# Moving the square root of the RMS norm to the start of ScalarE's next step in a fused attention and MoE kernel

## The reference

```python
h = _layernorm(x) * (1 + ca) + sa
x = x + ga * attn(h)            # linear attention with decay, 16 heads of 16
h = _layernorm(x) * (1 + cb) + sb
x = x + gb * ffn(h)             # shared gated MLP + top 2 of 8 experts

# attn, after the block recurrence over n has made o:
o = o * rsqrt(mean(o * o, axis=-1) + 1e-6)
o = u * o
return o @ W_out.T
```

## Time and profile before

| | |
|---|---|
| median of 3 runs | 375.64 us (375.27 to 375.65) |
| profiled execution, its own time | 375.64 us |
| its span | 373.8 us |
| TensorE busy | 362.9 us, 97% |
| VectorE, ScalarE, GpSimd busy | 280.2, 218.6, 200.8 us |
| granted TensorE clock | 1.0 of full speed throughout |

### The profile page before, as it was taken

The page is one execution under the profiler, slowest core; times in us unless marked ns, Lnnn a source line. Parts: engine busy times, 40 slices in busy tenths (PEclk is TensorE's granted clock), DMA queues, the critical chain, the costliest instruction groups (busy, mean ns, idle before and its releaser), DMA issues.

```text
span 373.8 us, 12932 instructions
## 1 busy us (share of the span) xinstructions
PE 362.9 (97%) x4978; PEld 315.0 (84%) x4983; DVE 280.2 (75%) x561; ACT 218.6 (58%) x453; POOL 200.8 (54%) x193
## 2 busy tenths in 40 slices
PE   8989998999999989999999999999999999999996
PEld 4546555778888769899999999999999999999995
DVE  7996388999899985579976987777777675555543
ACT  5688667677677755648276746555555634333222
POOL 2000003978778785311364687868767787674240
PEclk9999999999999999999999999999999999999999
DMA  8956031000197007999425465574685865665443
GB/s 265 375 63 60 2 134 37 2 4 30 32 353 184 31 31 265 330 336 271 88 92 108 104 110 104 95 118 88 104 109 91 100 101 103 100 114 77 70 58 113
DMA packets 53043, 45.35 MB, mean 121 GB/s; under 512 B 31524, under 2 KB 46996, under 8 KB 52856
## 3 DMA queue, kind: packets, MB, share of 16 engines
q1 hardware_dynamic: 43048, 32.09, 32.5%
q0 software_dynamic: 7488, 10.27, 18.2%
q10 hardware_dynamic: 2448, 2.18, 1.8%
HBM read 27.60 MB, written 10.49 MB: 102 GB/s over the span
## 4 chain that ended last, share of the span: by engine, by line
PE 72%; POOL 13%; DVE 7%; issue 5%; ACT 3%; ACTq 0%; POOLq 0%; DVEq 0%
PE ps L1630 37%; PE ps L1648 18%; PE ps L1413 7%; POOL tmp L554 3%; POOL tmp L558 2%; POOL tmp L575 2%; PE ps L1399 2%; POOL h2s L579 2%; POOL tmp L573 2%; POOL wx L563 2%; PE ps L1341 2%; DVE st L937 1%; PE ps L1533 1%; PE ps L1361 1%; DVE tmp L1254 1%
## 5 line engine op out<-in xcount | busy, mean ns | idle before, releaser
L1630 PE MATMUL ps<-tmp,wx 128*128 128x128 bf16 x1776 | 105.5, 219 | 0.0
L1630 PEld LDWEIGHTS ps<-tmp,wx 128*128 (+1 forms) x1776 | 102.3, 98 | 0.9 <-issue 0.2
L611 POOL DMA_INDIRECT out<-tmp,dk x39 | 72.0, 1846 | 38.0 <-SPq L515 32.5
L857 ACT ACTIVATE tmp<-tmp 128x512 bf16<-128x512 f32 x55 | 34.6, 629 | 80.8 <-PE ps L1648 61.6
L1648 PE MATMUL ps<-wx,tmp 128*128 (+1 forms) x660 | 80.7, 273 | 0.2 <-DVE tmp L1260 0.2
L1648 PEld LDWEIGHTS ps<-wx,tmp 128*128 128x128 bf16 x660 | 62.2, 98 | 6.9 <-DVE tmp L1260 0.5
L1254 DVE TENSOR_TENSOR tmp<-ps,tmp 128x512 f32<-128x512 f32 x55 | 37.9, 689 | 37.7 <-PE ps L1630 32.1
L1630 PE MATMUL ps<-w_hl,wx 128*128 128x128 bf16 x864 | 51.3, 219 | 0.9 <-ACT tmp L846 0.9
L606 POOL DMA_INDIRECT tmp<-h2rows,src_i x39 | 42.1, 1081 | 16.7 <-issue 10.8
L1630 PEld LDWEIGHTS ps<-w_hl,wx 128*128 (+1 forms) x864 | 49.6, 98 | 1.4 <-issue 1.0
L1260 DVE TENSOR_TENSOR tmp<-tmp 128x512 bf16<-128x512 f32 x55 | 38.3, 696 | 10.1 <-ACT tmp L857 9.9
(11 more groups left out here) (194 smaller groups left out, 555.2 us busy)
## 6 DMA issues: line engine op xcount, KB each, us to landing
wx<-in_wexp SPq DMA_DIRECT2D x26, 512.0 KB, 5.4
xres<-in_x SPq DMA_DIRECT2D x4, 512.0 KB, 6.6
h2rows<-h2s ACTq DMA_DIRECT2D x16, 128.0 KB, 3.4
out<-h2s SPq DMA_DIRECT2D x12, 128.0 KB, 2.1
h2s<-in_wmod SPq DMA_DIRECT2D x1, 1024.0 KB, 9.5
wx<-decay_rows SPq DMA_DIRECT2D x16, 64.0 KB
modr<-mod_rows SPq DMA_DIRECT2D x1, 1024.0 KB, 4.4
wx<-in_wqkvu SPq DMA_DIRECT2D x1, 768.0 KB, 6.8
```

The lines of the kernel that those rows point to most:

```text
L611: e.indirect_dma_start(t["out"], bass.IndirectOffsetOnAxis(ap=dst_i[:, j:j + 1], axis=0), yb[(NA + j) % 2], None, compute_op=ALU.add).then ...
L857: e.activation(hs[p][:, 0:FF], hf[p], ACT.Copy).then_inc(s["inner_high"], 1)
L1630: ins = e.matmul(half(bank, m * P), weight(at_, weights(part, w) + k * FF + m * P, P), xT[f % NXT][:, (2 * a + k) * P:(2 * a + k + 1) * P] ...
```

## The change

In ScalarE's step the RMS root leaves its place between L766 and L774 and becomes the first instruction of the next step. It treats tile m = n-3 there, where it treated tile m + 1 = n-2 at the end of the step before; the order in which the tiles are treated, the semaphore and its counts stay.

```diff
             def step_attention(n):
                 m, h, v, l = n - 3, n - 4, n - 1, n - 5
+                if mine(m):
+                    wait(e, "out_product", m + 1)
+                    e.activation(rs2[:, m % 2, 0:1], half(OUT_BANK, D, 1), ACT.Sqrt, scale=1.0 / D, bias=epst[:, 1:2]).then_inc(s["rms_root"], 1)
                 if mine(l):
                     wait(e, "logit_product", l + 1)
                     e.activation(logit[:, tile_of(l)[0], :], half(H_BANK, D, NE), ACT.Copy).then_inc(s["logits_taken"], 1)
...
                     e.activation(h2T[:, h % 2].rearrange("p k n -> p (k n)"), half(H_BANK, 0, D), ACT.Copy).then_inc(s["h2_taken"], 1)
-                if mine(m + 1):
-
-                    wait(e, "out_product", m + 2)
-                    e.activation(rs2[:, (m + 1) % 2, 0:1], half(OUT_BANK, D, 1), ACT.Sqrt, scale=1.0 / D, bias=epst[:, 1:2]).then_inc(s["rms_root"], 1)
                 if mine(m):
                     wait(e, "ln2_shift", m + 1)
                     wait(e, "h2_made", m - 1)
```

## The result

The changed kernel takes 380.67 us (median of 4, 380.44 to 381.49) against 375.64 us before (median of 4, 375.27 to 375.95). The ratio is 1.0139, interval 1.0122 to 1.0154: 5.0 us slower. The forecast was 380.5.

What follows compares the result with a forecast made beforehand. TensorE was taken to set the attention pace at 5.21 us a step; the start's 0.55 us and longer two-engine rings delayed attention's end by 5.0 us, so 375.64 + 5.0 = 380.6, rounded down to 380.5, range 377.4 to 382.5.

Steps and rivals of the forecast that it cites:

- What holds the normalisation: ScalarE's L774 waits for VectorE's L1116, so moving the root starts it no earlier, except at n = 16 (up to 0.69 us).
- The ring: Loop VectorE's step, normalisation, moved root, reciprocal: 5.30 us a plain attention step against TensorE's 5.21.
- with the copy: Ring in steps where ScalarE's 128x1024 copy L789 stands between normalisation and root: 0.94 us more, 6.24 us.
- with the long subtraction: Steps with VectorE's own 128x1024 subtraction L1124, where that is the longer way: 5.85 us.
- the hand-over: From ScalarE's root to VectorE's reciprocal: 0.04 us; at 0 the loss falls 0.3 us, at 0.10 it grows 0.5.
- The table load: First root's 1.28 us load at the start now stands behind the copy, making L1081 0.55 us later; no further drain counted.
- The step n = 3 to 4: L1081 to L1081 was taken to last 6.01 us as before, since VectorE's L1124 decides there.
- The long L1116: VectorE's shift, mostly 0.16 us, once 0.46: long in each of twelve steps adds 3.6 us, in a third 1.2.
- The passing on: Attention's delay reaches TensorE through GpSimd's rows, and everything behind attention moves as a block: +5.0 us.
- Partly absorbed: Rival: in the attention steps only the direct hits, 0.55 at the start and three copies, count: 378.0 us; chance 0.10.
- Faster: Rival: ScalarE's in-order wait holds L774, so rows and TensorE's turn come earlier: 372.2 us at best; chance 0.07.
- The root never stalled: Rival: ScalarE reaches the moved root before TensorE's product is done, so the stall merely moves; would give the 378.0 us case.

Runs made afterwards that it cites:

- e5: Changed kernel with the root moved further back, behind the logit copy and the two query masks: 395.22 us, ratio 1.0508 to the kernel before.
- e4: Changed kernel with ScalarE's shared copy moved ahead of the row normalisation, into its wait for VectorE's shift: 378.02 us, ratio 1.0059 to the kernel before.
- e3: Kernel before with only ScalarE's shared copy moved, from behind the normalisation to ahead of the root: 376.30 us, ratio 1.0011.
- e1: Changed kernel with the moved root directly behind the normalisation and ahead of the shared copy: 377.78 us, ratio 1.0056 to the kernel before.
- e6: Changed kernel with only the first root (n = 2) at its old place ahead of the shared copy: 380.83 us, ratio 1.0123 to the kernel before.
- e7b: Kernel before with only VectorE's last shared subtraction moved from n = 14 to n = 16: 376.28 us, ratio 1.0006.
- e8b: Kernel before with VectorE's last shared subtraction at n = 16 and TensorE's wait for it moved to the first shared product: 378.39 us, ratio 1.0011.
- e8: Kernel before: root behind normalisation at n = 15 and 16, VectorE's last subtraction at n = 16, TensorE's wait for it at first shared product: 378.82 us, ratio 0.9999.

## Why the prediction was right

- **What holds the normalisation.** Right. Freed of the root, it still starts when VectorE's shift is done, at each of 14 steps. No step got its rows earlier, except at n = 16 against the first shared product (0.68 us ahead of it, before 0.09), and there it gave nothing, as assumed: from that product to the end it is 231.7 us against 231.6.
- **The ring.** 5.30 forecast, 5.29 measured; with the copy 6.24 and 6.24; with the long subtraction 5.85 and 5.86. The root took 0.24 and not 0.26, the hand-over 0.03 and not 0.04. The bounds that I kept for the hand-over weren't needed. Nor was the one for a long L1116: the longest L1115 took 160 ns, so the chain did not meet that stall. e5 raised the ring by 1.29 us and e4 took the copies out of it, and the periods came out as worked out.
- **The table load.** Before n = 3, 0.56 us as worked out: 70.18 - 64.89 = 5.29 against 69.89 - 65.16 = 4.73. ScalarE's rows show no further drain, neither ahead of the load nor behind it, against what the Trainium skill (ScalarE: Activation LUTs, What ACT_TABLE_LOAD costs) adds:

```profile
67.52 1.06 ACT L788 ACTIVATE wx<-h2s 128x1024 bf16<-128x1024 f32 x1
68.59 1.28 ACT L737 ACT_TABLE_LOAD   x1
69.89 0.26 ACT L737 ACTIVATE rs<-ps,epst 128x1 f32<-128x1 f32 x1
```

- **The step n = 3 to 4.** Off by 0.14: I carried over 6.01 us, and it took 76.05 - 70.18 = 5.87. That is most of the 0.18 by which the stretch came out under the forecast (4.86 against 5.04). The 6.01 held a long L1116, 0.31 us, which began under a GpSimd instruction and ended with it; in the change VectorE came after that instruction's end. Before, and then the change:

```profile
73.22 1.27 POOL L589 TENSOR_TENSOR h2s<-h2s,modr 128x512 f32<-128x512 f32 x1
...
74.19 0.31 DVE L1116 SCALAR_TENSOR_TENSOR rs<-mv,rs 128x1 f32<-128x1 f32 x1
```

```profile
72.93 1.27 POOL L589 TENSOR_TENSOR h2s<-h2s,modr 128x512 f32<-128x512 f32 x1
...
74.50 0.16 DVE L1115 SCALAR_TENSOR_TENSOR rs<-mv,rs 128x1 f32<-128x1 f32 x1
```

  The step is 5.86 to 5.87 us in all three kernels in which only the table load makes it late (the change, e3, e4), with 0.16 us there, and 5.99 to 6.02 in all nine with the load at its old time, with 0.29 to 0.31. So the table load's net price is 0.4 us, the 0.56 less this.
- **The long L1116.** Read wrongly: it was not long once. Four of its sixteen took more than 0.2 us before (0.31, 0.46, 0.21, 0.22), none in the change. I had feared more such stalls in the longer chain, and there were fewer.
- **The passing on.** Right. TensorE waits at the end for GpSimd's rows, as before, and nothing behind attention absorbs or adds:

```profile
144.74 0.41 PE L1518 MATMUL ps<-kept,tmp 128*128 128x128 f32 x2 [0.98 <-POOL tmp L558]
...
146.80 1.50 PE L1629 MATMUL ps<-tmp,wx 128*128 128x128 bf16 x24
```

- **The rivals.** Partly absorbed would be 378.0 by direct hits alone; e1 shows that the plain rings count too. Faster fell with the first point. The root never stalled for TensorE. The case for a faster kernel was also read from one step: L774 starts 0.30 us behind L770 in the plain steps about n = 9, but between 0.15 and 1.05 over all.

By parts, from the attention steps: plain rings 1.7 us (e1), table load 0.4 (e4 less e1; e6 agrees), three copies 2.8 (the change less e4), together 4.9. These are differences in a row from one kernel to the next, so they add up by construction; what checks them is e6's 0.41 for the table load, and the periods in the timelines.

## What to carry to other kernels

Before taking an in-order wait away, ask what the instructions behind it wait for. If those are released at the same moment by another engine, nothing starts earlier, and the moved instruction may now lie behind that engine's last result and ahead of its first one: a ring between two engines, whose length is to be added up and held against the pace of the engine that sets it. Idle time in front of an instruction is where other work can be hidden (e4); it isn't by itself a cost, and emptying another part of the ring need not gain anything either (e3).

## What the runs showed of the hardware

VectorE and GpSimd lengthened each other's instructions, by the order in which they began.

- *VectorE first.* GpSimd's 128x256 shift L558 took 0.73 us, and 1.71 us when it began 0.07 us behind VectorE's 128x1024 subtraction of two SBUF operands (e7b; 1.70 in e8b). That is 1.0 us on a path that TensorE waited for, and it undid what e7b let through. Begun 0.8 us behind such a subtraction, GpSimd's L554 took 1.01 to 1.03 us (three times in the kernel before, four in the change).
- *GpSimd first.* In e8 L558 began 0.57 us ahead of the subtraction and took its usual 0.73. VectorE's 128x1 shift, 0.16 us alone, took up to 0.50 us when it began under a GpSimd instruction, and ended 0.01 to 0.02 us after it (n = 3 before, n = 12 and 14 in e3). Not each time: at 100.64 in the kernel before it began under one with 0.12 us left and took 0.16.

The Trainium skill (SBUF — State Buffer, SBUF: two separate sides) says that a VectorE instruction with two SBUF inputs and a GpSimd instruction that reads SBUF exclude each other on a shared pair of ports for the whole instruction, whichever starts first. The rows agree in kind. By this rule alone e7b's L558 would have taken 1.12 + 0.73 = 1.85 us, by my estimate from its rows; it took 1.71.
